# Token lists of a mixture-of-experts stage: the operand layout of VectorE's 2048-element passes, with the token group innermost

## What is computed

```python
scores = softmax(xf @ gate_w.T)          # 16384 tokens, 8 experts
vals, idx = top_k(scores.T, 2048)        # each expert takes its 2048 best tokens
y = layernorm(xf[idx]) * ln_w + ln_b
h = gelu(y @ fc1.T + b1)                 # 256 -> 1024, per expert
out = (h @ fc2.T + b2) * vals
xf = xf.at[idx].add(out)
```

## Time and profile before

| what | us |
|---|---|
| median of three runs (4479.81 to 4485.28) | 4482.48 |
| the profiled execution, its own time | 4495.45 |
| its span, first to last instruction | 4493.7 |
| stage 1 / stage 2 / stage 3 with its prologue / stage 4 | 3413 / 113 / 870 / 98 |
| stage 3: start to first expert matmul (3525.7 to 3579.2) | 53.5 |
| busy over the span: PE, DVE, ACT, POOL | 3641.8, 3903.1, 3456.2, 3513.4 |
| mean granted TensorE clock, as a share of full speed | 0.897 |

### The profile page before, as it was taken

One profiled execution on the slowest core, in us unless ns is written; L12 is line 12 of the kernel. 1 busy time (PEld: TensorE's weight loads), 2 busy tenths in 40 slices (PEclk: granted clock), 3 DMA queues, 4 the chain that ended last, 5 costly groups with the idle time before them and its releaser, 6 DMA issues. The chain is left out here.

```text
span 4493.7 us, 57414 instructions
## 1 busy us (share of the span) xinstructions
PE 3641.8 (81%) x19154; PEld 2548.8 (57%) x19154; DVE 3903.1 (87%) x4971; ACT 3456.2 (77%) x5860; POOL 3513.4 (78%) x1714
## 2 busy tenths in 40 slices
PE   7888888888888888888888888888753299999990
PEld 3455555555555555555555555555542288888880
DVE  4999999999999999999999999999984777677645
ACT  5888988888888888888988988888860156565655
POOL 3889999998999899999988999899870266666543
PEclk8889999999999999999998999999865599999995
DMA  2666666665666666666666666666642133333328
GB/s 74 142 146 159 156 153 158 157 160 144 153 154 155 152 163 155 151 163 149 152 150 150 155 156 157 154 155 159 144 113 35 52 60 74 63 62 60 65 30 304
DMA packets 179904, 594.77 MB, mean 132 GB/s; under 512 B 33424, under 2 KB 99088, under 8 KB 128160
## 3 DMA queue, kind: packets, MB, share of 16 engines
q0 software_dynamic: 70368, 335.06, 38.6%
q1 hardware_dynamic: 104640, 239.32, 15.5%
q10 hardware_dynamic: 4608, 16.78, 0.9%
HBM read 221.47 MB, written 68.68 MB: 65 GB/s over the span
## 5 line engine op out<-in xcount | busy, mean ns | idle before, releaser
L433 POOL TENSOR_TENSOR dbu<-du,bb 128x2048 f32<-128x2048 f32 x512 | 2399.6, 4721 | 219.9 <-DVE h L793 190.1
L793 DVE TENSOR_TENSOR_SCAN h<-da,hlast,dbu 128x512 f32<-128x512 f32 x1536 | 1876.6, 1266 | 30.7 <-POOL dbu L433 19.7
L485 ACT ACTIVATE da<-dl,negA 128x512 f32<-128x512 f32 x2048 | 1397.6, 693 | 217.1 <-DVE h L793 213.6
L719 PE MATMUL ht<-ident,h 128*128 128x128 f32 x8192 | 1228.0, 299 | 341.0 <-ACT pair L504 178.0
L719 PEld LDWEIGHTS ht<-ident,h 128*128 128x128 f32 x8192 | 1026.8, 154 | 755.8 <-DVE h L793 324.6
L793 DVE TENSOR_TENSOR_SCAN h<-da,dbu 128x512 f32<-128x512 f32 x512 | 594.5, 1206 | 14.1 <-ACT da L485 10.1
L504 ACT ACTIVATE pair<-ht,ct 128x512 f32<-128x512 f32 x768 | 512.7, 682 | 88.1 <-PE ht L719 85.9
L649 PE MATMUL spare<-xin,win 128*128 128x512 f32 x1024 | 496.0, 615 | 14.4 <-DVE conv L773 12.0
L655 PE MATMUL spare<-xh,conv 128*128 128x512 f32 x1024 | 463.1, 595 | 1.5 <-ACT dl L518 0.8
L801 DVE SCALAR_TENSOR_TENSOR pair<-ht,ct,pair 128x512 f32<-128x512 f32 x544 | 394.3, 730 | 59.8 <-PE ht L719 59.8
L1202 POOL DMA_INDIRECT sums<-ot,idx x128 | 221.8, 1733 | 167.2 <-DVE ot L1491 138.0
(11 more groups left out here) (165 smaller groups left out, 5730.9 us busy)
## 6 DMA issues: line engine op xcount, KB each, us to landing
acc<-pair POOLq DMA_DIRECT2D x192, 1024.0 KB, 7.3
bb<-b_rows SPq DMA_DIRECT2D x128, 1024.0 KB, 5.1
acc<-acc POOLq DMA_DIRECT2D x64, 1024.0 KB, 8.6
dl<-du POOLq DMA_DIRECT2D x62, 512.0 KB, 7.7
xin<-in_xt SPq DMA_DIRECT2D x32, 512.0 KB, 8.3
xres<-in_x SPq DMA_DIRECT2D x32, 512.0 KB, 8.8
x_scores<-xres SPq DMA_DIRECT2D x32, 512.0 KB, 3.0
sums<-xres SPq DMA_DIRECT2D x32, 512.0 KB, 4.1
```

The lines of the kernel that those rows point to most:

```text
L433: pool.tensor_tensor(dbu[n % 2][:], du[q][:], bb[part % 2][:, m:m + 1, :].to_broadcast([P, DT, CH]), ALU.mult).then_inc(dbu_done, 1)
L485: act.activation(da[DA_SLOT[m]][:], dl[q][:, dt, :], ACT.Exp, scale=negA[:, dt, n:n + 1]).then_inc(exp_done, 1)
L719: last = te.transpose(ht[HT_SLOT[m]][:, dt * P:(dt + 1) * P], h[n % 2][:, dt, b * P:(b + 1) * P], ident[:])
L793: dve.tensor_tensor_scan(h[n % 2][:, dt, :], da[DA_SLOT[n * DT + dt]][:], dbu[n % 2][:, dt, :], start, ALU.mult, ALU.add).then_inc(scan_do ...
```

## The change

The four tiles count, isin, rhs and onehot get the group g as their innermost dimension: count becomes [128, 128, 16] (each number 16 times), isin [128, 8, 16, 16] with g last, rhs [128, 8, 2, 16, 16], and onehot [128, 128, 16]. In the passes "hi", "blk" and "lo" are then repeated in a middle or outer dimension, and every operand has a step of one element in its innermost dimension. The list matmuls read the onehot and rhs of a group with a step of 16 elements (32 bytes). The wide count is written by two engines: VectorE the numbers 0 to 15, and ScalarE the numbers 16 to 127, in a copy put ahead of its table load, with a new semaphore that VectorE waits for ahead of its first onehot. The number of passes, matmuls and DMAs, and their order, stay.

```diff
--- before.py
+++ after.py
@@ -1045,7 +1045,7 @@
         a = Alloc(nc, ctx)
         ident = a.sb("ident3", [P, P])
         counti = a.sb("counti", [P, P], I32)
-        count = a.sb("count", [P, P], BF16)
+        count = a.sb("count", [P, P, G], BF16)
         blki = a.sb("blki", [P, SL, G], I32)
         blk = a.sb("blk", [P, SL, G], BF16)
         pidi = a.sb("pidi", [P, 1], I32)
@@ -1059,9 +1059,9 @@
         b1 = [a.sb(f"b1_{i}", [P, FM]) for i in range(2)]
         b2 = a.sb("b2", [P, E, 256])
         ln = a.sb("ln", [P, 2, 2])
-        isin = a.sb("isin", [P, SL, G, 16], BF16)
-        rhs = a.sb("rhs", [P, SL, G, 2, 16], BF16)
-        onehot = [a.sb(f"onehot{i}", [P, G, P], BF16) for i in range(OH)]
+        isin = a.sb("isin", [P, SL, 16, G], BF16)
+        rhs = a.sb("rhs", [P, SL, 2, 16, G], BF16)
+        onehot = [a.sb(f"onehot{i}", [P, P, G], BF16) for i in range(OH)]
         idxf = a.sb("idxf", [P, 16])
         idx = [a.sb(f"idx{i}", [P, NT], I32) for i in range(2)]
         xg = [a.sb(f"xg{i}", [P, 4, 264]) for i in range(4)]
@@ -1089,6 +1089,7 @@
         added = [S(f"rows_added{t}") for t in range(NG)]
         st, var_ok, rstd_ok, xn_ok = S("stats3_steps"), S("variance3"), S("rstd3_ready"), S("xn_ready")
         shift_ok = S("shift3_ready")
+        consts_wide = S("wide_count_ready")
         tp_ok, yt_ok = S("turned3"), S("yt_ready")
         f1_ok, gelu_ok, f2_ok = S("fc1_done"), S("gelu_done"), S("fc2_done")
         idxf_ok = S("idxf_ready")
@@ -1232,6 +1233,8 @@
 
             @block.scalar
             def _(act):
+                act.wait_ge(iotas, 1)
+                act.copy(count[:, 16:P, :], counti[:, 16:P].unsqueeze(2).to_broadcast([P, P - 16, G])).then_inc(consts_wide, 1)
                 act.preload_act_table_set("gelu_apprx_tanh_and_others")
 
                 def normalise(grp, r):
@@ -1294,8 +1297,8 @@
                         if s == 0:
                             te.wait_ge(rhs_ok, 3 * e + 3)
                         for g in range(G):
-                            last = te.matmul(lists[:], onehot[s % OH][:, g, :],
-                                             rhs[:, s, g].rearrange("p a t -> p (a t)"),
+                            last = te.matmul(lists[:], onehot[s % OH][:, :, g],
+                                             rhs[:, s, :, :, g].rearrange("p a t -> p (a t)"),
                                              start=s == 0 and g == 0, stop=s == SL - 1 and g == G - 1)
                         last.then_inc(oh_used, 1)
 
@@ -1361,8 +1364,9 @@
             @block.vector
             def _(dve):
                 dve.wait_ge(iotas, 3)
-                for dst, src in ((count, counti), (blk, blki), (pid, pidi)):
-                    dve.tensor_copy(dst[:], src[:]).then_inc(consts, 1)
+                wide = counti[:, 0:16].unsqueeze(2).to_broadcast([P, 16, G])
+                for dst, src in ((count[:, 0:16, :], wide), (blk[:], blki[:]), (pid[:], pidi[:])):
+                    dve.tensor_copy(dst, src).then_inc(consts, 1)
                 dve.wait_ge(consts, 3)
 
                 def list_rhs(e):
@@ -1371,20 +1375,22 @@
                     if e > 0:
                         dve.wait_ge(oh_used, e * SL)
                         dve.wait_ge(rhs_ok, 3 * e)
-                    dve.tensor_tensor(isin[:], hi.unsqueeze(3).to_broadcast([P, SL, G, 16]),
-                                      count[:, 0:16].unsqueeze(1).unsqueeze(1).to_broadcast([P, SL, G, 16]),
+                    dve.tensor_tensor(isin[:], hi.unsqueeze(2).to_broadcast([P, SL, 16, G]),
+                                      count[:, 0:16, :].unsqueeze(1).to_broadcast([P, SL, 16, G]),
                                       ALU.is_equal).then_inc(rhs_ok, 1)
                     dve.wait_ge(rhs_ok, 3 * e + 1)
-                    dve.tensor_tensor(rhs[:, :, :, 0, :], isin[:], blk[:].unsqueeze(3).to_broadcast([P, SL, G, 16]),
+                    dve.tensor_tensor(rhs[:, :, 0], isin[:], blk[:].unsqueeze(2).to_broadcast([P, SL, 16, G]),
                                       ALU.mult).then_inc(rhs_ok, 1)
-                    dve.tensor_scalar(rhs[:, :, :, 1, :], isin[:], pid[:, 0:1], None, ALU.mult).then_inc(rhs_ok, 1)
+                    dve.tensor_scalar(rhs[:, :, 1], isin[:], pid[:, 0:1], None, ALU.mult).then_inc(rhs_ok, 1)
 
                 def list_onehot(e, s):
                     if e > 0 or s >= OH:
                         dve.wait_ge(oh_used, e * SL + s - OH + 1)
                     lo = d["lo"][:, s, bass.ds(e, 1), :].rearrange("p a g -> p (a g)")
-                    dve.tensor_tensor(onehot[s % OH][:], lo.unsqueeze(2).to_broadcast([P, G, P]),
-                                      count[:].unsqueeze(1).to_broadcast([P, G, P]), ALU.is_equal).then_inc(oh_ok, 1)
+                    if e == 0 and s == 0:
+                        dve.wait_ge(consts_wide, 1)
+                    dve.tensor_tensor(onehot[s % OH][:], lo.unsqueeze(1).to_broadcast([P, P, G]), count[:],
+                                      ALU.is_equal).then_inc(oh_ok, 1)
 
                 def list_index(e, p):
                     dve.wait_ge(oh_used, (e + 1) * SL)
```

## The result

The median is 4517.28 us against 4483.19 us before, both over four runs: a ratio of 1.0074, 95% interval 1.0061 to 1.0086. The kernel became slower by 34 us, 5 us outside the range.

What follows compares the result with a forecast made beforehand. TensorE was taken to bound the expert stage and VectorE its prologue. The terms -10.7 - 2.1 + 0.1 + 1.8 + 0.4 = -10.5 us gave a forecast of 4472.0 us, range 4467 to 4512.

Steps and rivals of the forecast that it cites:

- What bounds the kernel: Expert stage: TensorE busy 99.99 of every 100 us from 3579.2 us on; VectorE's gain paid out only in the prologue.
- Part 1: VectorE's two-source passes fall from 2284 to 1221 ns; in the prologue -10.7 us, and -2.1 us through POOL's waits.
- Rival C: VectorE's passes gain nothing, TensorE's price stays: about 4485 us, chance 0.05.
- the rule that was cited: VectorE: two-source passes pack 16-bit pairs when every operand's innermost step is 1; a repeated element falls to the slow rate.
- Part 2: Prologue: VectorE's wider first cast costs +0.1 us; ScalarE's copy, at most 2.4 us, stays hidden with 1.5 us to spare.
- Part 3: TensorE's list matmuls with 32-byte steps: +2 ns a pair, +1.8 us in the stretch and +0.4 us in the prologue.
- rival A: TensorE's list matmuls pay the hop in time: 61 ns a pair, 4503 us, chance 0.36 with its one-stream form.
- The distance: First expert matmul to end of TensorE's work: unchanged by the forecast, which is wrong if it grows over 4 us.
- the forecast's own range: Total time of the forecast case alone, with the ends of VectorE's price and the POOL term: 4465 to 4476 us.
- the one-stream form: TensorE reads the 128 weights in one stream, 122 ns: about 4556 us, chance 4%, counted within rival A.

Runs made afterwards that it cites:

- q2: The kernel before with only the onehot changed, two groups innermost, so the weights step by 4 bytes: 4473.23 us, ratio 0.9977.
- w_only: The kernel after with isin and rhs laid out as before, so only the weights hop 32 bytes: 4515.21 us, ratio 1.0065.
- q8: q2 with eight groups innermost in the onehot, so the weights step by 16 bytes: 4523.76 us, one run.
- q4: q2 with four groups innermost in the onehot, so the weights step by 8 bytes: 4477.87 us, one run.

## Why the prediction was wrong

**What bounds the kernel: right.** The expert stretch is TensorE's, the prologue VectorE's. VectorE's 67.5 us less in the stretch brought nothing.

**Part 1, VectorE: right in each term.** 1218 to 1224 ns for the two-source passes (1221 taken), the scalar pass unchanged at 746, -12.1 us in the prologue for -12.3. Rival C falls with that, and the fast pass of q2 confirms it: it is the repeated innermost element that held the passes at 2284 ns. This agrees with the rule that was cited.

**Part 2, the wide count: right.** Hidden; 1.68 us, below the bound of 2.4.

**Part 3, TensorE: the step that failed.** It reads: "If the same halving holds for TensorE in its own cycles, the 13 ns become 26: the pace rises by some 1 to 2 ns." The term for the stretch was +1.8 us; the stretch grew by 46.7. The hop is not paid in TensorE's cycles. Hopping pairs start 60 ns apart at the 1.2 GHz level and 60 at 2.4 (moving operand alone), and about 63 and 65 with both operands: the clock doubles and the pace stays. The hop is paid in time, and rival A had the size: 1.9 ns for each element of a stream, read from VectorE's hopping pass, gives 61 ns; the moving operand alone measured 58.9, the weights alone 61.6. (For the 128 weights the figure fits only if four of them are read at a time, as the rival supposed; no run here shows that by itself.) I had the row and the right figure from it, and gave them 0.36 because I assumed the slack of a fast array to be slack of its reads. The Trainium skill (Advanced Engine Details and Errata, SBUF Cachelines) named a mechanism that fits; the table above agrees with it for TensorE, but for one point. It asks for at least two hits on a line; with two, the pair took 33 ns in place of 25, and the measurement decides.

**Why rival A, too, came out short** (4503 against 4517): its pace was 61 for 65 (3.6 us), and it had no term for the clock. The 10.9 us that the pace leaves are the larger part of the miss, and without them the time would lie inside the range; nearly all of them (10.6) went with the long runs and their dips. A longer list run was priced as if the matmuls around it kept their speed.

**Signs that were named.** The distance was to stay within 4 us if the forecast held; it grew by 46.7. That sign alone would have told the case.

Two sums of the prediction are slightly off and change nothing: the low end of the forecast's own range comes to 4466, not 4465, and the 4556 of the one-stream form leaves out what the prologue's slabs would add.

## What to carry to other kernels

A layout belongs to its writer and to its readers: a step that lets one engine pack pairs makes another hop, and the price is paid on the reader's engine, so ask first which of the two is saturated. Interleave only as far as the writer needs (here two elements, 4 bytes), and keep four elements that are read in turn on each 16 bytes; both engines then ran at their full rate here. Slack that is measured in an engine's clock says nothing about the time of its reads.

## What the runs showed that was not expected

- A run of 64 list pairs at 65 ns each, with TensorE never idle by its busy time (4.00 of 4.00 us), ends in most cases with a fall of the granted clock from 2.4 to 1.2 GHz for 3.4 us; a run of 32 never did. Cutting the runs returned 10.6 of 845.1 us at an unchanged pace. Why slow pairs do this while TensorE shows as busy stays open.
- The slow reads of the two operands overlap: 61.6 ns and 58.9 ns alone, 65 ns together.
- Two POOL operations on 4 elements per partition took 2.06 and 2.24 us beside VectorE's two-source passes and 1.00 and 1.17 us beside the shorter ones: they end with the pass, at either of its rates.
- The prologue's pairs seem to take 70 ns; that is VectorE's pace of one slab in 1.13 us. w_only and q8 show the same 70 ns there, though their own paces are 62 and 60.
- Why q4's pace is 33 ns stays open.
